# A four-stage transformer kernel: work ordered in quarter slots, queries and keys emptied from PSUM by VectorE, sigmoid as tanh

## The reference, cut to what matters

```python
# stage 1: 6 layers of attention with a band of 126 keys, then an FFN
for l in range(LAYERS):                       # 6
    q, k, v = x @ Wq.T + bq, keys @ Wk.T + bk, keys @ Wv.T + bv   # 16 heads of 8
    attn = softmax(where(valid, q . k / sqrt(8), neg))
    x = _ln(x + (attn @ v) @ Wo[l].T + bo[l], ln1_g[l], ln1_b[l])
    x = _ln(x + gelu(x @ W1[l].T + b1[l]) @ W2[l].T + b2[l], ln2_g[l], ln2_b[l])
# stage 2: token mixing
out = sigmoid(xr @ W_r.T) * (square(relu(xk @ W_k.T)) @ W_v.T)
# stage 3: one causal attention over blocks of 512, keys weighted by a phase gate
# stage 4: a router picks 3 of 8 experts for each sequence
zone = sum over the 3 experts: w[e] * (gelu(x @ Wa[e]) @ Wb[e])
```

## Time and profile before

| | |
|---|---|
| median of 3 runs | 1345.5 us (1343.86 to 1346.16) |
| the profiled execution | 1351.89 us |
| its span in the profile | 1350.1 us |
| mean granted TensorE clock | 0.921 of full speed |
| busy: PE, DVE, ACT, POOL | 1058.2, 804.8, 779.0, 404.6 us |
| share of the chain that ended last | PE 44%, ACT 15%, DVE 14%, POOL 8%, issue 8%, SP's queue 7%, DMA 4% |

### The profile page before, as it was taken

The page is one execution under the profiler, slowest core; times in us unless marked ns, Lnnn a source line. Parts: engine busy times, 40 slices in busy tenths (PEclk is TensorE's granted clock), DMA queues, the critical chain, the costliest instruction groups (busy, mean ns, idle before and its releaser), DMA issues.

```text
span 1350.1 us, 46954 instructions
## 1 busy us (share of the span) xinstructions
PE 1058.2 (78%) x20080; PEld 730.1 (54%) x20080; DVE 804.8 (60%) x2451; ACT 779.0 (58%) x1419; POOL 404.6 (30%) x544
## 2 busy tenths in 40 slices
PE   1466989889898888987989889878656778887835
PEld 0244666666666666665666666656434434544524
DVE  2456667666666677765766666675477765543111
ACT  5144656666666665655666666666445657566532
POOL 4313233332223333322333232333445242202020
PEclk9777999999999999998999999988768879989968
DMA  4211212213211211231221321110201023010110
GB/s 130 47 50 50 50 50 50 51 50 85 47 41 39 79 39 46 50 85 50 50 51 50 85 47 41 41 34 3 48 2 48 7 45 96 10 49 10 48 55 8
DMA packets 72626, 64.79 MB, mean 48 GB/s; under 512 B 16226, under 2 KB 66914, under 8 KB 72418
## 3 DMA queue, kind: packets, MB, share of 16 engines
q1 hardware_dynamic: 72418, 61.78, 17.9%
HBM read 15.70 MB, written 1.05 MB: 12 GB/s over the span
## 4 chain that ended last, share of the span: by engine, by line
PE 44%; ACT 15%; DVE 14%; POOL 8%; issue 8%; SPq 7%; DMA 4%; POOLq 0%; ACTq 0%; DVEq 0%
PE s L530 5%; DVE mx L1008 4%; PE d L647 4%; PE a L511 4%; ACT probs L802 4%; SPq L1492 4%; PE d L730 3%; PE a L430 3%; DMA qpack<-mrows 3%; PE a L637 2%; PE a L719 2%; PE d L545 2%; PE d L430 2%; PE d L557 2%; SPq L1499 2%
## 5 line engine op out<-in xcount | busy, mean ns | idle before, releaser
L802 ACT ACTIVATE probs<-a 128x443 f32<-128x443 f32 (+2 forms) x736 | 358.3, 538 | 273.6 <-PE a L511 270.5
L1008 DVE TENSOR_REDUCE mx<-d 128x2 f32<-128x378 f32 (+1 forms) x768 | 346.8, 510 | 101.3 <-PE d L464 101.2
L530 PE MATMUL s<-probs,vals 128*32 128x189 f32 (+5 forms) x3968 | 191.4, 318 | 14.7 <-ACT probs L802 14.5
L530 PEld LDWEIGHTS s<-probs,vals 128*32 128x32 f32 x3968 | 122.2, 111 | 56.0 <-ACT probs L802 20.1
L511 PE MATMUL a<-qpack,kpack 64*64 64x189 bf16 (+4 forms) x3968 | 143.1, 243 | 0.0
L430 PE MATMUL d<-band,identb 64*64 64x252 bf16 x1152 | 89.5, 301 | 54.1 <-DVE mx L1008 44.4
L464 PE MATMUL d<-kpack,qpack 62*64 62x189 bf16 (+1 forms) x3072 | 128.3, 243 | 0.0
L430 PE MATMUL a<-band,identb 64*64 64x252 bf16 x1152 | 85.0, 285 | 47.3 <-DMA qpack<-mrows 32.0
L1005 DVE TENSOR_REDUCE mx<-d 128x1 f32<-128x512 f32 (+7 forms) x256 | 98.4, 447 | 30.5 <-PE d L479 30.3
L1334 POOL TENSOR_SCALAR veps<-mv 128x4 f32<-128x4 f32 x48 | 11.0, 228 | 327.4 <-DVE mv L1109 327.3
L637 PE MATMUL a<-xmid,w 128*128 128x512 f32 x192 | 94.5, 617 | 4.6 <-ACT hid L880 4.6
(11 more groups left out here) (180 smaller groups left out, 1940.4 us busy)
## 6 DMA issues: line engine op xcount, KB each, us to landing
kpack<-kparts SPq DMA_DIRECT2D x168, 128.2 KB, 3.0
qpack<-qparts SPq DMA_DIRECT2D x168, 128.0 KB, 3.1
qpack<-mrows SPq DMA_DIRECT2D x224, 4.0 KB
w<-in_w SPq DMA_DIRECT2D x12, 256.0 KB, 3.9
w<-in_wa SPq DMA_DIRECT2D x12, 256.0 KB, 3.3
w<-in_wb SPq DMA_DIRECT2D x12, 256.0 KB, 3.5
rowt<-in_rowt SPq DMA_DIRECT2D x6, 384.0 KB, 3.4
stream<-in_x SPq DMA_DIRECT2D x4, 256.0 KB, 4.0
```

The costliest lines, as they stand in the source:

```text
L530: mm = pe.matmul(s_ps[32 * j:32 * j + 32, q0:q0 + w - skip], vals[:, u % 2, at:at + 32], probs[:, n % SETS, j, col + skip:col + w], start= ...
L802: act.activation(probs[:, n % SETS, j, 0:width], a_ps[A.bank("exp", u, v, b)][:, 0:width], ACT.Exp, scale=SCALE).then_inc(a_emptied, 1)
L1008: red = dve.tensor_reduce(out[:, 2 * tb:2 * tb + 2], bank[:, 0:2 * width].rearrange("p (t k) -> p t k", k=width), AX.X, ALU.max)
```

## The change

Six things are changed.

- The slot is cut into four steps (`STEPS` = 64 for a unit), and each kind of job has a step of its own. Everything of a tail is 1 to 2 slots earlier than before: `turn_sums` at step 150 (37.5 slots, before 39), `second` at 195 (48.75, before 50). The maxima keep slots 8 to 23, the scores lie a quarter slot later.
- The keys are projected before the queries, at steps 0 and 2.
- Queries and keys: DVE alone reads the bank, adds the bias and writes a float sum (`biased`); ACT casts the sum to the high part; POOL makes the rest by a subtraction of its own and then the middle and the low part as before. `lower` has three POOL instructions in place of two, and stands two steps after `biased` in the loop.
- `second` and the experts' matmuls are written in four parts (`f`); the parts of `second` have one step, those of the experts' second matmul two.
- Even values no longer wait for odd ones; a bank that held values is taken when both have read it (`take_d`).
- The last layer's turned output (`turn_norm(u, 1)` for units 20 to 23), which nothing read, is left out. The sigmoid is `0.5 * (1 + tanh(x / 2))`, with the 0.5 in the square of the keys.

```diff
+FIRST = 32
+CAUSAL_FIRST = (1605, 1683, 1763, 1843)
+QUERIES = (2, 2)
+KEYS_AT = (0, 12)
+SPLIT_LAG = 1
+MAX_AT, MAX_STEP = (32, 32), (4, 4)
+PARTS_LAG = 4
+EXP_AT, EXP_STEP = (93, 93), (4, 4)
+HEADS_AT = ((150, 182), (150, 182))
+FFN = (195, 195, 195, 195)
+ROOT2 = 195
...
             def biased(u, name):
...
+                dve.wait_ge(d_filled, D.n(name, u))
+                dve.tensor_scalar(total[:, first:], d_ps[D.bank(name, u)][:, :], bias, None, ALU.add
+                                  ).then_inc(d_emptied, 1)
...
             def high(u, name):
+                act.wait_ge(d_emptied, D.n(name, u))
...
+                act.copy(parts[:, 0, :], source[:, :]).then_inc(done, 1)
...
             def lower(u, name):
-                pool.wait_ge(d_emptied, D.n(name, u))
+                pool.wait_ge(hi, u + 1)
+                pool.tensor_tensor(rest[:, :], total[:, :], parts_[:, 0, :], ALU.subtract).then_inc(done, 1)
+                pool.wait_ge(done, u + 1)
                 pool.tensor_copy(parts_[:, 1, :], rest[:, :]).then_inc(mid, 1)
                 pool.wait_ge(mid, u + 1)
                 pool.tensor_tensor(parts_[:, 2, :], rest[:, :], parts_[:, 1, :], ALU.subtract).then_inc(lo, 1)
...
-                for u in due(g, QP):
+                for u in due(g - 2 * SPLIT_LAG, QUERIES):
                     lower(u, "q")
-                for u in due(g, KP):
+                for u in due(g - 2 * SPLIT_LAG, KEYS_AT):
                     lower(u, "k")
...
-                for u in banded_due(g, TAIL[0] + FFN):
+                for u in banded_due(g, ROOT2):
                     root(u, 1)
...
-                act.activation(rgate[:, :], a_ps[A.bank("mixr", b)][:, :], ACT.Sigmoid).then_inc(a_emptied, 1)
+                act.activation(xr[:, :], a_ps[A.bank("mixr", b)][:, :], ACT.Tanh, scale=0.5
+                               ).then_inc(a_emptied, 1)
```

More of the change, by code:

```diff
@@ L1 @@
+import collections
+import functools
 from contextlib import ExitStack
@@ L105, in before, with held @@
         return self.place[job] - self.depth
+    def held(self, *job):
+        return self.jobs[self.before(*job) - 1] if self.before(*job) > 0 else ("none",)
 def base(u):
-    return BASE + SLOTS * u if u < UNITS else CAUSAL0 + CSLOTS * (u - UNITS)
+    return FIRST + STEPS * u if u < UNITS else CAUSAL_FIRST[u - UNITS]
 def causal(u):
     return u >= UNITS
-def due(g, at, late=None):
-    late = at if late is None else late
-    return [u for u in range(ALL) if base(u) + (late if causal(u) else at) == g]
@@ L122, in banded_due @@
[L122 to L144, removed]
@@ L147, in sums_due, with tiles_of, calendar @@
[L147 to L156, removed]
 def banks_of(u):
     return len(CAUSAL_BANKS) if causal(u) else len(CHUNK_BANKS)
+def tiles_of(u):
+    return len(CAUSAL_TILES) if causal(u) else TILES
+def calendar(days):
+    out = collections.defaultdict(list)
+    for step, what in days:
+        out[step].append(what)
+    return out
@@ new lines, in unit_days, with due, banded_due, causal_due @@
+@functools.lru_cache(None)
+def unit_days(banded, late):
+    return calendar((base(u) + (late if causal(u) else banded), u) for u in range(ALL)
+                    if (late if causal(u) else banded) is not None)
+def due(g, at):
+    return unit_days(*at).get(g, ())
+def banded_due(g, at):
+    return unit_days(at, None).get(g, ())
+def causal_due(g, at):
+    return unit_days(None, at).get(g, ())
+@functools.lru_cache(None)
+def maxima_days():
+    return calendar((base(u) + MAX_AT[causal(u)] + MAX_STEP[causal(u)] * n, (u, *divmod(n, tiles_of(u))))
+                    for u in range(ALL) for n in range(LANES * tiles_of(u)))
@@ L163, in set_of, with sums_due, parts_step, parts_days @@
+def sums_due(g):
+    return sum_days().get(g, ())
+def parts_step(u, half):
+    return base(u) + MAX_AT[causal(u)] + MAX_STEP[causal(u)] * 2 * tiles_of(u) * (half + 1) + PARTS_LAG
+@functools.lru_cache(None)
+def parts_days(lag):
+    return calendar((parts_step(u, half) + lag, (u, half)) for u in range(ALL) for half in range(2))
+def parts_due(g, lag):
+    return parts_days(lag).get(g, ())
 def set_of(u, group, b):
@@ L793, in _ @@
+                for f in range(CHUNKS):
+                    for b, r in experts_due(g, OUT_E[f]):
+                        expert_out(b, r, f)
         @block.scalar
@@ L1256, in _ @@
             for g in range(TOTAL):
-                for half in range(2):
-                    for u in due(g, MAX0 + 8 + 8 * half, MAX0 + 10 + 10 * half):
-                        parts(u, half)
+                for u, half in parts_due(g, -PARTS_LAG):
+                    parts(u, half)
                 for u, couple, tb in maxima_due(g):
@@ L1275, in _ @@
                     take_phase(u)
[L1276 to L1279 removed]
+                for half in range(2):
+                    for u in due(g, HEADS_AT[half]):
+                        normalise_heads(u, half)
+                for u in banded_due(g, OUT[0]):
                     residual(u, 0)
[L1281 removed]
+                for u in banded_due(g, FFN[-1]):
```

532 lines of the change are left out of this document (275 added, 257 removed).

## The result

The changed kernel takes 1413.3 us (median of 4 runs, 1407.7 to 1418.3) where the kernel before took 1345.8 (1343.9 to 1348.9) on the same chip: ratio 1.050, 95% interval 1.045 to 1.055. The forecast was 1430 with a range of 1365 to 1485. The profiled execution has a span of 1408.8 us, 58.7 more than before.

The account below looks back on a forecast made before the run. PE was taken to bound the periods, with the DMA chain to the first scores setting the new first stretch. +92 (21 periods) + 3 (units 0 to 2) - 10 (last part) = +85 us: median 1345.5 to 1430, range 1365 to 1485.

Parts of the forecast that it names:

- the order does what it is built for: Rival: all waits at the first scores go, 34.9 us a period, 1310 us in all; chance 0.12.
- loses nothing: Rival "nothing measurable": chain of about 11 us to the first scores, removed waits pay for the new one, 1345 us; chance 0.04.
- the root doesn't hold up the queries: Rival: queries' parts made in time, only two packs in a row count; chain about 12.3 us, 1375 us; chance 0.06.
- what PE does meanwhile: FFN's end to first scores: PE needs 10.4 us (6.2 + 3.7 + 0.5) and waits 4.4 of the 14.8.
- the sign of being right: At the first scores PE waits for the DMA of `mrows`, 3.5 to 5.5 us, 21 times.
- the periods: FFN's end to FFN's end: 40.5 us (39.3 to 41.8) against 36.1, +4.4 each, +92 us over 21.
- the constants of stage 3: Within the 20 periods: a cost of 5 us, paid once before and once again after.
- The second stretch: First scores to next FFN's end: shrinks from 28.7 to 24.5 us (24.0 to 24.7).
- The clock: Behind the wait at the first scores: a slow clock costs 1.2 us (1.0 to 1.3) in each of 21 periods.
- The last part: From 877.4 us on: -10 us (0 to -25), with earlier tails, four table loads and four turnings gone.
- the cast on ACT: At the queries and keys: ACT reads SBUF in place of the bank, no change.
- The rival with the two packs in a row: Same case as "the root doesn't hold up the queries": period 38.0 us, +40 in all, 1375 us; chance 0.06.

Follow-up runs that it names:

- e1: Kernel after with POOL's root of the FFN's variance moved behind the queries' parts: 1387.2 us, ratio 1.028 to the kernel before.
- e2: Kernel after with the maxima's DMAs ahead of the queries' pack in SP's queue, POOL's order unchanged: 1368.7 us, ratio 1.013 to the kernel before.
- e3: Kernel after with the edits of e1 and e2 together: 1358.5 us, ratio 1.007 to the kernel before.
- b3: b1 with two added products of 128x512 floats on POOL right behind the root of the FFN's variance: 1379.6 us, ratio 1.024 to the kernel before.
- e6: Kernel after with keys and queries projected 4 steps earlier, both packs ahead of the maxima's DMAs, sums turned 3 steps later: 1397.5 us, ratio 1.036.
- b4: b1 with the sigmoid as tanh and without the last layer's turning: 1327.7 us, ratio 0.985 to the kernel before.
- e7: Kernel after with keys and queries projected 4 steps earlier and the queries' pack behind the maxima's DMAs: 1369.8 us, ratio 1.016 to the kernel before.
- b2: b1 with the new split alone (DVE sums, ACT casts, POOL three instructions): 1352.5 us, ratio 1.003 to the kernel before.
- e9: Kernel after with keys projected at step -12, queries at -8, packs issued when ready ahead of the maxima, sums turned at 153: 1383.2 us, ratio 1.026.
- b1: Kernel before with the maxima's DMAs ahead of both packs in SP's loop: 1327.1 us, ratio 0.982 to the kernel before.
- b5: b1 with the same two POOL products as b3, but behind the residue of the FFN's output: 1341.5 us, ratio 0.995 to the kernel before.

## Why the prediction came out as it did

**Right: that it gets slower, by about how much, and where.** The queries' parts behind the root, then the pack, then the maxima set the first scores. By its steps, in the period shown: root's end 3.50 us after the FFN's end (3.48 forecast), POOL's three 3.06 (3.2), from the pack's start to the first scores 7.47 (8.1). The mean is 14.6 us, forecast 14.8. e1 and e2 each take one link out and win 26 and 45 us, e3 both and 55. The cases in which the order does what it is built for, or loses nothing, are out, and so is the one in which the root doesn't hold up the queries: their subtraction starts when the root ends.

**Wrong: what PE does meanwhile.** I had PE arrive at 10.4 us and wait 4.4 for the DMA. The DMA wait is 1.1 to 2.2 us in 18 of 20 periods and less in two; I named 3.5 to 5.5 as the sign of being right, and under 2 us as one of being wrong, which 12 of the 20 are. The sum of the waits there is nearly right (4.8 us in the period shown, forecast 4.4 and 0.5), and that is no proof of the working: with the chain setting the stretch, the waits add up to what PE's own work leaves of it, however they are shared out. The step that failed is the list of what PE waits for: 1.31 us for `ztok`, which POOL holds up (b3), and 0.83 us for the sums, whose turning now comes right behind the last sums and ahead of ACT's copy, were not in it, and the wait for `otok` was put at 0.51 us and is 0.89. The working had DVE's waits there "cost nothing any more" and took no account of POOL's new instructions beside DVE's `ztok`, behind the root. While the chain sets the time, the short waits cost nothing extra (e6). They are why e2 alone, with 12.7 us in most periods, doesn't reach the forecast's 10.4.

**The term that was too large: the periods.** 20 of them were to cost 88 us more and cost 65. Of the 23 us between, 9 are the constants of stage 3. I put them at 5 us in both kernels; before, their period has 44.6 us, 9 more than those around it, with a wait of PE of 3.90 us for DVE and a slow clock behind it, and after it has 40.2, no more than its neighbours. The other 14 are 0.7 a period. The second stretch is 24.95 us in the mean instead of 25.7, since without a slow clock it is 23.85, just below the lower bound of 24.0: 15 us. The first is 0.24 shorter: 5 us. Against that, an ordinary period of before is 35.8 and not 36.1 us: 6 us the other way. A part of that is a plain error, as the base was cut at 150.20, while unit 0's FFN ends at 148.51 + 3.84 = 152.35; the 20 periods are 725.0 and not 727.2 us. FFN's ends 39.3 to 41.8 us apart were the sign; the mean of 39.5 lies in it, and 7 of the 20 periods, those with the full clock, last 37.9 to 38.1.

**The clock.** 1.2 us in each of 21 periods was forecast. It was 1.4 to 2.4 us in 13 of 20, a mean of 1.1, so the term is right in size by luck: fewer slow clocks than forecast, and longer ones. The rule of the Trainium skill that I had weighed (TensorE: Matmul & The Clock Gate, HAM oscillation) holds for about two turns in three here. 7 waits of 1.2 to 1.4 us were followed by a clock of 1.00, and in 5 of the 13 periods the clock had fallen before the wait for the transfer began. With waits of 1.9 to 3.5 us, in e6, it was every turn.

**The last part.** The 8.2 us won behind unit 20's FFN's end hold the 21st period of the sum, which grew by 4.1 us (43.3 to 47.4, forecast 4.4). So the last part is 12.3 us shorter, where -10 was forecast, but not for one of the reasons given: table loads and turnings weigh nothing measurable (b4). After and every e kernel but e7 have 460 to 467 us there, before 472.7, so it comes with something that they share, the new places of the tails or of the causal units or another of the edits; which, wasn't tried. The start lost 1.6 us (3 were put down for units 0 to 2). With 65.3 in the 20 periods that makes the 58.7 us, where the working has 85.

**Costed at nothing, and not so: the cast on ACT.** "DVE's waits for ACT go" was right, "no change" for ACT was not. ACT now waits for DVE: 0.8 us a period in b2, where the gelu stands behind the cast. In after the gelu stands ahead of both casts, and ACT idles 2.68 us behind them (from 548.75 on, in the period shown), so the wait of 0.45 us for the queries' sum costs nothing there. In e9, where the gelu is behind again, it comes out.

**Slips that the sum doesn't rest on.** The first stretch before has 6.9 us in the mean and not 7.4. The rival with the two packs in a row comes to 1345.5 + 40 - 7 = 1378 us, not 1375, and the bounds of the terms give about 1390 to 1470 for the forecast's own range, not 1393 to 1474. 10.6 against 5.1 us of table loads would be 5.5 us, not 5 at most.

**What stays open.** e3 lies 1.8 us a period above b1. The traces name the parts (the pack of the queries up to 1.7 us, and 1.0 a period in the mean; sums 0.8; `otok` 0.9 against 0.7), but no run removed them all. The new split was tried in the old order alone, so what it costs in the new one isn't shown, and neither the matmuls in four parts nor the values' banks (`take_d`) were tried by themselves. A version with the new order, early projections, early weights and the old split wasn't run.

## To carry to other kernels

Before an order is rebuilt for short waits, look at the one queue that all the late data passes: here moving four DMAs ahead of twelve in SP's loop gave 1.8%, and of the 67 us that the rebuilt order lost 45 came back when the four were moved ahead of six (e2). When a wait between two engines is turned round, read what stands in the queue of the engine that will wait from then on. And a wait in the profile hides the ones behind it: taking it away gives its full length only if nothing else is late behind it. In e6 shorter waits for the sums made the one for the DMA longer, and in e7 a wait for the queries came where that for the maxima had gone. Before work is moved on POOL, look at what DVE does at that time.

## What the hardware did that I had not expected

- VectorE's `TENSOR_SCALAR` from SBUF to SBUF stands still while a GpSimd instruction works on SBUF, and one gets through where the next GpSimd instruction follows: four of 128x128 floats take 1.1 us alone, 2.7 beside two GpSimd products (b3), 3.1 beside three instructions (after, e2); one of 128x32 takes 0.93 instead of 0.17 us (b5). Those that read PSUM keep their lengths: the maxima have 509 ns in the mean in b5 and 510 in b1, `otok` 424 and 425.
- Equal waits of PE were followed by different clocks: 1.23 us before 326.95 and 564.87 in the kernel after, then 1.00 and 0.55 over the next 3.6 us. So it is with the 1.75 us in e9: 1.00 and 0.50.
- Without the wait at the first scores the kernel runs in a strict rhythm: 17 of b1's 20 periods differ by 0.01 us, those of before by up to 3 us.
